# Six-pass graph network on one core: the attention passes' pipeline reordered to two slots a group, with two gathers fewer a pass

## What is computed

```
h = relu(layernorm(x));  q, k, v = h @ Wq + bq, h @ Wk + bk, h @ Wv + bv
a   = einsum(q[src], k[dst]) / sqrt(D)          # one score a head and edge
ex  = exp(a - segment_max(a, dst)[dst])
agg = segment_sum(v[src] * ex, dst) / segment_sum(ex, dst)
x   = x + prelu(layernorm(gate * skip + (1 - gate) * agg))
```

## Time and profile before

| | |
|---|---|
| median of 3 runs | 6951.99 us (6948.68 to 6959.38) |
| the profiled execution | 6951.92 us |
| its span | 6950.0 us |
| TensorE / weight loads / VectorE busy | 71% / 59% / 69% |
| ScalarE / GpSimd busy | 22% / 68% |
| granted TensorE clock, mean | 0.786 |

### The profile page before, as it was taken

How to read it: one execution, slowest core, us unless ns; L and a number is a source line. 1 busy time by engine, 2 the same in 40 slices (tenths; PEclk the granted TensorE clock), 3 DMA queues, 4 the chain that set the end, 5 groups by cost and what they waited for, 6 DMA issues and landing times. The chain is left out here.

```text
span 6950.0 us, 92236 instructions
## 1 busy us (share of the span) xinstructions
PE 4911.1 (71%) x26631; PEld 4085.5 (59%) x26631; DVE 4761.2 (69%) x14309; ACT 1562.0 (22%) x4929; POOL 4755.9 (68%) x5008
## 2 busy tenths in 40 slices
PE   2655555667766577777688888867888886667766
PEld 2444444556665465565466666656777775566665
DVE  4444443777877577877577777747777874788786
ACT  2433332222222111111112112111222221121121
POOL 3777776777776577777577666627777763777774
PEclk8666666777677788888799889968887886877776
DMA  4444445666666355555455555547766673666664
GB/s 133 165 164 158 159 164 146 204 216 210 214 217 180 125 161 167 166 155 167 121 171 179 167 164 175 168 121 228 242 229 229 231 219 134 215 226 220 223 226 138
DMA packets 408006, 1267.81 MB, mean 182 GB/s; under 512 B 128774, under 2 KB 189958, under 8 KB 321110
## 3 DMA queue, kind: packets, MB, share of 16 engines
q1 hardware_dynamic: 200000, 760.73, 30.7%
q0 software_dynamic: 200240, 496.31, 25.8%
q10 hardware_dynamic: 7270, 4.88, 0.3%
HBM read 1084.56 MB, written 176.98 MB: 182 GB/s over the span
## 5 line engine op out<-in xcount | busy, mean ns | idle before, releaser
L756 POOL DMA_INDIRECT gathered_rows<-table_l,arena x3056 | 2909.3, 952 | 1192.4 <-issue 904.2
L1298 PE MATMUL ps<-weighted_rows,onehot 128*128 128x136 f32 (+2 forms) x8320 | 1527.4, 341 | 573.9 <-DVE acc L1150 568.8
L1298 PEld LDWEIGHTS ps<-weighted_rows,onehot 128*128 128x128 f32 x8320 | 1353.3, 241 | 729.3 <-DVE weighted_rows L1139 334.1
L1260 PEld LDWEIGHTS ps<-dst_side,onehot_t 128*128 128x128 f32 x8320 | 1299.9, 232 | 384.1 <-issue 318.3
L756 POOL DMA_INDIRECT gathered_rows<-table_l,src_rel_edges x1120 | 1063.7, 950 | 603.5 <-issue 328.4
L1260 PE MATMUL ps<-dst_side,onehot_t 128*128 x8320 | 1381.4, 320 | 90.0 <-DVE products L1067 43.8
L1150 DVE TENSOR_TENSOR acc<-acc,ps 128x136 f32 (+2 forms) x4160 | 1185.9, 285 | 178.1 <-PE ps L1298 83.5
L1256 PE MATMUL ps<-gathered_rows,ident 128*128 128x512 f32 x832 | 547.3, 745 | 307.0 <-DMA gathered_rows<-table_l,arena 302.4
L1072 DVE TENSOR_REDUCE scores<-products 128x16 f32<-128x512 f32 (+2 forms) x1040 | 706.5, 679 | 10.0
L879 PE MATMUL ps<-gathered_rows,onehot 128*128 128x128 f32 x1664 | 346.3, 373 | 465.3 <-ACT gathered_rows L816 464.3
L756 POOL DMA_INDIRECT arena<-table_l,src_rel_edges x544 | 516.5, 950 | 180.2 <-issue 160.3
(11 more groups left out here) (322 smaller groups left out, 6029.5 us busy)
## 6 DMA issues: line engine op xcount, KB each, us to landing
onehot_t<-onehots_turned SPq DMA_DIRECT2D x260, 1024.0 KB
onehot<-onehots SPq DMA_DIRECT2D x260, 1024.0 KB
onehots<-onehot SPq DMA_DIRECT2D x52, 1024.0 KB, 6.8
onehots_turned<-onehot_t SPq DMA_DIRECT2D x52, 1024.0 KB, 4.3
table_l<-arena SPq DMA_DIRECT2D x50, 1024.0 KB
gathered_rows<-table_l,arena POOLq DMA_INDIRECT x3056, 2.5
segment_flags_sb<-segment_flags SPq DMA_DIRECT2D x1300, 8.2 KB
arena<-type_mask_rows SPq DMA_DIRECT2D x75, 256.0 KB
```

The source lines that it names most:

```text
L756: pool.indirect_dma_start(out=home(v, t // GC)[:, t % GC, :], out_offset=None, in_=table, in_offset=bass.IndirectOffsetOnAxis(ap=index[:, ...
L1260: ins = nc.tensor.matmul(ps[:, BZ + k, g * P:(g + 1) * P], e.ohT[:, u, t * P:(t + 1) * P], kRows[:, bass.ds(bs[t % 8], D)], start=not gat, ...
L1298: ins = nc.tensor.matmul(ps[:, BP + n % 3, at:at + PW], e.oh[:, u, t, :], exvT[:, t, :], start=True, stop=True)
```

## The change

- A group passes through two slots and the beginning of a third. VectorE's slot s holds the products and scores of group s, and of group s-1 the chain, maxima, rescale, weighing and adds 0 to 10; adds 11 to 15 of a group stand at the start of the next slot. The flag `weighs` and one drain slot go.
- ScalarE's `open_scale`, `exps` and `exp_columns` stand in a row, without a hook between them, and TensorE's `spread_drop` and `turn_back` likewise.
- TensorE forms all four chunks of destination rows of group s in slot s; if `gat`, the identity matmul of the gathered rows comes last and in a function of its own (`own_rows`), further down the list.
- `first(k)` becomes 8 (s + 1) + 6 for t < 11 and 8 (s + 2) otherwise.
- The last group gathers 14 tiles in place of 16; waits for its rows are lowered by as much.
- Register loads of eight places, two a slot on each of the two engines, as before; VectorE's second one is kept over to the next slot.

```diff
+LACK = NT - NT_MAX
+ON_TIME = SUMMED[3][1]
...
+def rows_wanted(s, j, q):
+
+    return 64 * (q + 1) - (16 * LACK if s == NG - 1 and j == J - 1 else 0)
+
...
-            for t in range(GT):
+            for t in range(min(GT, NT_MAX - s * GT)):
...
                     keep_scores(s - 1)
                 after.act(act, x)
-                after.act(act, x + 1)
                 if cur:
                     keep_column(s, u, q)
-                after.act(act, x + 2)
-                after.act(act, x + 3)
+                after.act(act, x + 1)
                 if chain:
                     open_scale(s - 1, 1 - u)
-                after.act(act, x + 4)
-                if chain:
                     exps(s - 1)
-                after.act(act, x + 5)
+                    exp_columns(s - 1)
+                after.act(act, x + 2)
+                for h in range(3, 7):
+                    after.act(act, x + h)
                 if cur:
                     keep_linear(s, w)
-                after.act(act, x + 6)
-                if chain:
-                    exp_columns(s - 1)
                 after.act(act, x + 7)
 
...
+            late_places = {}
+
+            def unit_of_adds(s, n, bs):
+                for t in range(*SUMMED[n]):
+                    add(s, t, bs[t % 8])
+
+            def slot(s, w, qw, cur=True, chain=True, late=True):
+
+                r, o = s - 1, s - 2
                 v, rq = two(*place(w, qw, ways, -1))
-                vp = (w - 2) % buffers
                 x = HOOKS * s
-                def late_adds(n, m):
-                    if late:
-                        for k in range(n, m):
-                            add(o, 8 + k, bb[k])
                 if late:
-                    bb = blocks_of(o, 8)
-                if late:
-                    e.p_ready.wait(dve, a_no, UNITS * (o + 1))
-                if weighs:
-                    e.excol_ready.wait(dve, a_no, p + 1)
-                    last_maxima(p)
-                    for j in range(J):
-                        weigh(p, vp, j)
-                after.dve(dve, x)
-                late_adds(0, 3)
+                    bo = late_places.pop(o)
+                    unit_of_adds(o, 4, bo)
                 if chain:
                     scan_tiles(r, v, rq)
-                late_adds(3, 5)
+                if late:
+                    unit_of_adds(o, 5, bo)
                 if chain:
                     turn_ends(r)
-                late_adds(5, 8)
+                after.dve(dve, x)
                 after.dve(dve, x + 1)
-                if weighs:
-                    bp = blocks_of(p, 0)
-                    rescale(p, w % 2, bp[0])
                 if chain:
                     chain_forward(r, v)
                 if cur:
                     product(s, w, qw, 0)
                 if chain:
                     chain_backward(r, v)
+                    hand_back_ends(r)
+                    open_drop(r)
+                    max_forward(r, v)
+                    max_backward(r, v)
+                    less_maximum(r)
+                if cur:
+                    score(s, 0)
                 if chain:
-                    hand_back_ends(r)
+                    br = blocks_of(r, 0)
+                    rescale(r, v, br[0])
                 after.dve(dve, x + 2)
                 if chain:
-                    open_drop(r)
-                if cur:
-                    score(s, 0)
-                if weighs:
-                    for t in range(3):
-                        add(p, t, bp[t])
+                    e.excol_ready.wait(dve, a_no, r + 1)
+                    last_maxima(r)
+                    for j in range(J):
+                        weigh(r, (w - 1) % buffers, j)
                 after.dve(dve, x + 3)
                 if cur:
                     product(s, w, qw, 1)
-                if weighs:
-                    add(p, 3, bp[3])
-                if cur:
                     score(s, 1)
+                if chain:
+                    unit_of_adds(r, 0, br)
                 after.dve(dve, x + 4)
                 if chain:
-                    max_forward(r, v)
-                    max_backward(r, v)
-                    less_maximum(r)
+                    unit_of_adds(r, 1, br)
+                    unit_of_adds(r, 2, br)
+                    bl = late_places[r] = blocks_of(r, 8)
                 after.dve(dve, x + 5)
-                if weighs:
-                    add(p, 4, bp[4])
                 if cur:
                     product(s, w, qw, 2)
-                if weighs:
-                    add(p, 5, bp[5])
-                if weighs:
-                    add(p, 6, bp[6])
-                if cur:
                     score(s, 2)
+                if chain:
+                    unit_of_adds(r, 3, bl)
                 after.dve(dve, x + 6)
-                if weighs:
-                    add(p, 7, bp[7])
                 if cur:
                     product(s, w, qw, 3)
                     score(s, 3)
@@ -1233,33 +1230,34 @@
...
+            slot(NG, NG % ways, NG // ways, cur=False)
+            slot(NG + 1, (NG + 1) % ways, (NG + 1) // ways, cur=False, chain=False)
...
             def dst_rows(s, w, qw, j, bs):
                 u, q = two(w, qw)
-                v, qv = buffer(w, qw)
                 c, k = J * s + j, j % 2
-                if gat:
-                    here[v][j].wait(pe, here_no, 64 * (qv + 1))
                 if not (static(s, 1) and j < 2):
 
                     e.prod_ready.wait(pe, a_no, c - 1)
-                if gat:
-
-                    nc.tensor.matmul(ps[:, BZ + k, :].rearrange("p (g d) -> p g d", d=D), e.ident[:, :], home(v, j)[:, :, 0:D],
-                                     start=True, stop=False)
                 for g in range(GC):
                     t = GC * j + g
                     ins = nc.tensor.matmul(ps[:, BZ + k, g * P:(g + 1) * P], e.ohT[:, u, t * P:(t + 1) * P],
-                                           kRows[:, bass.ds(bs[t % 8], D)], start=not gat, stop=not gat or g == GC - 1)
-                ins.then_inc(e.z_ready.sem, 1)
+                                           kRows[:, bass.ds(bs[t % 8], D)], start=not gat or g == 0, stop=not gat)
+                if not gat:
+                    ins.then_inc(e.z_ready.sem, 1)
+
+            def own_rows(s, w, qw, j):
+                v, qv = buffer(w, qw)
+                if gat:
+                    here[v][j].wait(pe, here_no, rows_wanted(s, j, qv))
+                    nc.tensor.matmul(ps[:, BZ + j % 2, :].rearrange("p (g d) -> p g d", d=D), e.ident[:, :], home(v, j)[:, :, 0:D],
+                                     start=False, stop=True).then_inc(e.z_ready.sem, 1)
...
-            def slot(s, w, qw, cur=True, chain=True, weighs=True, ahead=True):
-
-                r, p = s - 1, s - 2
-                u, pq = two(*place(w, qw, ways, -2))
-                wn, qn = place(w, qw, ways, 1)
+            def slot(s, w, qw, cur=True, chain=True):
+
+                r = s - 1
+                u, q = two(w, qw)
+                v, rq = two(*place(w, qw, ways, -1))
                 x = HOOKS * s
+                if cur:
+                    bs = blocks_of(s, 0)
+                    e.oht_here[u].wait(pe, a_no, 16 * (q + 1))
+                    dst_rows(s, w, qw, 0, bs)
+                if chain:
+                    turn_scores(r)
+                if cur:
+                    dst_rows(s, w, qw, 1, bs)
                 after.pe(pe, x)
-                if weighs:
-                    e.oh_here[u].wait(pe, a_no, 16 * (pq + 1))
+                if cur:
+                    own_rows(s, w, qw, 0)
+                after.pe(pe, x + 1)
+                if chain:
+                    spread_drop(r)
+                    turn_back(r)
+                after.pe(pe, x + 2)
                 if cur:
                     bs = blocks_of(s, 8)
-                if weighs:
-                    sums(p, u, 0)
-                after.pe(pe, x + 1)
-                if weighs:
-                    sums(p, u, 1)
-                    sums(p, u, 2)
-                after.pe(pe, x + 2)
-                if chain:
-                    spread_drop(r)
-                if cur:
                     dst_rows(s, w, qw, 2, bs)
                 after.pe(pe, x + 3)
-                if weighs:
-                    sums(p, u, 3)
+                if cur:
+                    own_rows(s, w, qw, 1)
+                if chain:
+                    e.oh_here[v].wait(pe, a_no, 16 * (rq + 1))
+                    for n in range(3):
+                        sums(r, v, n)
                 after.pe(pe, x + 4)
                 if cur:
                     dst_rows(s, w, qw, 3, bs)
+                if chain:
+                    sums(r, v, 3)
                 after.pe(pe, x + 5)
+                if cur:
+                    own_rows(s, w, qw, 2)
+                if chain:
+                    sums(r, v, 4)
+                    sums(r, v, 5)
                 after.pe(pe, x + 6)
```

(32 more changed lines are left out.)

29 lines of the change are left out of this document (14 added, 15 removed).

## The result

The changed kernel takes 7031.03 us (median of 4 runs, 7022.54 to 7034.22) against 6954.85 (6948.68 to 6959.38): a ratio of 1.0106, 95% interval 1.009 to 1.0122. It is slower by 76 us, where the forecast was 37 us faster, and it lies a microsecond above the range. The profiled execution is the fastest of the four, 7022.54 us with a span of 7020.8, 70.8 more than before.

What follows compares the result with a forecast made beforehand. GpSimd's gathers bound passes 1, 2 and 5, the VectorE, TensorE and ScalarE loop passes 3 and 4, with pass ends a second cost. Terms -10 - 96 + 10 + 0 + 59 = -37 us: 6952 to 6915 us, range 6790 to 7030.

Steps and rivals of the forecast that it cites:

- Two gathers fewer: Last group of a pass: rows come 2.5 us earlier in passes 0, 1, 2 and 5, -10 us; nothing in 3 and 4.
- One slot fewer at each end: End of passes 1 to 5, last product to last block's first read: 20 us each, -96 us in all.
- Adds and scores not interleaved: VectorE's slot: grouped adds and back-to-back scores cost 0.6 us more, hidden under the gathers in passes 1, 2 and 5.
- The sum: VectorE's work and waits added up per slot: pass 3 22.9 us, no change; pass 4 22.7, taken as 22.4.
- Exponentials without block work between: ScalarE and TensorE between maxima and weighing: about 1.3 us, covered by 1.4 to 1.6 of VectorE's work; costed at nothing.
- The drain that the prediction weighed and left out: ScalarE's table switch for the square root: about 1.38 us on top of the load, up to 58 us more in all.
- Destination rows ahead, own rows behind: Passes 2 and 3: one-hot part formed before gathered rows arrive, identity matmul closes the bank; same matmuls, costed at nothing.
- Block work in TensorE's list: Passes 3 and 4: projections and relations delay sums and scores; pass 4 slots 22.4 us, +59 us, pass 3 unchanged.
- the walk: Step-by-step count of pass 4's waits for sums and scores, all additive: 2.9 us a slot for 18 blocks, 1.8 for 7.
- the loop held by TensorE's list in every pass: Rival: each block-work matmul becomes a wait, passes 1, 2 and 5 at 20.6 us a slot; +96, 7048 us; chance 0.27.

Runs made afterwards that it cites:

- run 7: Changed kernel with the own rows' identity matmul opening the bank again and two adds put back between the third product and its score: 6888.29 us.
- run 2: Changed kernel with one part undone: the own rows' identity matmul opens the bank again, ahead of the one-hot matmuls: 6952.31 us.
- run 5: Changed kernel with twelve more one-hot matmuls a slot in passes 2 and 3, ahead of the spreading of the drop: 6992.22 us.
- run 10: The kernel of run 7 with pass 4's block work one place later for blocks whose last tile is below 11 in its group: 6857.28 us.
- Run 12: The kernel of run 10 with pass 4's key, value and query matmuls cut to the first of eight types: 6806.25 us.
- run 6: The kernel of run 2 with pass 4's block work shifted four to six places, to where TensorE waits for the drop: 6984.24 us.
- run 3: Changed kernel with two of VectorE's adds put back between the third product and its score: 7058.19 us.

## Why the prediction was wrong

1. *Two gathers fewer.* -2.5 us a pass was expected; pass 0 takes 1076.7 to 1084.9 us over the twelve runs and the changed kernel, and 1086.4 in the one trace of the kernel before. The sign fits; the size can't be told apart from that scatter. Not tried by itself.

2. *One slot fewer at each end.* Right. VectorE's timeline, last product and last block's first read, passes 1 and 4, as in the earlier trace rows:

```profile
2230.51 0.69 DVE L1076 TENSOR_TENSOR products<-gathered_rows,ps 128x512 f32<-128x512 f32 x1 [0.92 <-DMA gathered_rows<-table_l,arena]
...
2248.11 0.17 DVE L1775 TENSOR_SCALAR row_scalars<-acc 128x4 f32<-128x4 f32 x1
...
5863.98 0.68 DVE L1076 TENSOR_TENSOR products<-gathered_rows,ps 128x512 f32<-128x512 f32 x1
...
5886.56 0.17 DVE L2254 TENSOR_SCALAR row_scalars<-acc 128x8 f32<-128x8 f32 x1
```

17.6 and 22.6 us; 18.0, 22.1 and 18.9 in passes 2, 3 and 5 (before 35.4, 44.5 and 38.6). Together 99 us where 100 was said, 105 less than before where 96 was said. Passes 1, 3 and 5 show it whole.

3. *Adds and scores not interleaved.* The sign was right; the place was the wrong question. VectorE's busy time a slot of pass 1 is 848.26/51.9 = 16.3 us against 15.5 before, 0.8 more where 0.6 was said, and it stayed under the gathers in passes 1 and 5 as the step had it. (The step reads the earlier trace rows wrong in one place: with an add between, product and score start 4507.87 - 4507.07 = 0.80 apart; 0.60 is the product's share of it. The 0.12 a score that it goes on with is right.) What it missed is what stands ahead of the second register load. The sum counted both loads as work; with own rows early, a product, two adds and a score in place of five adds ahead of that load are worth 26 and 24 us in passes 3 and 4 (run 7), and the idle time that goes is the one behind the load. This is read from the waits; a kernel with only the load moved was not tried.

4. *Exponentials without block work between.* Right: VectorE's wait for ScalarE's columns during the gathers of pass 4 is 1.4 us, where it was 59.9. A square root stands ahead of the exponentials in this stretch of ScalarE's timeline:

```profile
5323.12 0.20 ACT L1476 ACTIVATE row_scalars<-row_scalars 128x1 f32<-128x1 f32 x1 [1.49 <-DVE row_scalars L1471]
5323.34 1.28 ACT L1023 ACT_TABLE_LOAD   x1
5325.25 0.27 ACT L1023 ACTIVATE open_node_scale<-ps,open_node_column 128x8 f32<-128x8 f32 x1 [0.62 <-PE ps L1274]
```

The load takes 1.28 us and ends 0.6 us before the spread drop comes, and the next activation starts 0.63 us after it. The drain that the prediction weighed and left out is longer than that, and is in no row; that the load is hidden here is read from this slot, and not tried by itself.

5. *Destination rows ahead, own rows behind: "I cost it at nothing".* **This step failed, by 52 us in pass 2 and 27.5 in pass 3** (run 2). I asked whether the gathered rows were there; they were. I did not ask when TensorE gets to the closing matmul, which stands in its list behind three things that VectorE and ScalarE release, and I took the matmuls to be "the same ones" in a place where they run at half the clock. GpSimd's pace was to cover pass 2, by 0.8 us a slot (19.3 under 20.1); the waits for the banks are 3.4 a slot (175.2/51), and the slot came out 1.3 over the gathers. That pass 3 came out right is luck. Its slot is 22.35 us as forecast, but without this part it is (4515.70 - 3408.22)/51 = 21.72 (run 2). VectorE's waits for banks, scores, scale and columns make some 3.6 us of the 22.35, where steps 5 and 6 had 2.7, so its own work is about 18.7 (an estimate from these waits), where the sum had 20.2: a wait left out and own work put too high cancelled. No row shows the 19.6 of that sum.

6. *Block work in TensorE's list.* The mechanism was right and its size too small: pass 4 slots of 23.63 us, not 22.4, +2.38 where +1.15 was said: 63 of the pass's 72 us. The own work in the sum, 20.1 us a slot, came out right: with the 3.6 us of waits below it makes 23.7. The two waits are where the step put them. It said 3.2 us for sums; the slot above shows 4.58. Over the pass, sums and scores make (140.7 + 44.7)/51 = 3.6 us a slot, and I had 2.6 from the walk and then took 0.3 off because a walk adds up what may overlap. One part of the difference is the clock: I took key and value at 3.84 us, they took 4.67 here, and 4.55 in the mean of the pass's 22 blocks with matmuls before the last gather (4.07 in the kernel before); the one-hot matmuls ahead of them took 2.07. The 0.3 off had no row behind it.

Of the rivals, the loop held by TensorE's list in every pass (7048) comes nearest in the total, but not in its passes: 1 and 5 never left the gathers' pace, at slots of 20.13 and 20.18, and 3 fell. It named the clock, which run 5 confirms for pass 2. What the forecast and this rival should have been is one case: new waits on TensorE's list in passes 2 to 4, and none that counts in 1 and 5. (Pass 5's busy time a slot, 813.65/51.9, is 15.7, not 15.6; nothing hangs on it.)

What stays open: after run 10, pass 4 is still 49 us longer than before, though its end is shorter. Run 12 puts a good part of that on the projections' total, and that VectorE's slot in the changed kernel has 0.8 us more work is measured; how the rest divides was not tried.

## What to carry to other kernels

When a step is split so that its first half goes ahead, price the second half where it now stands: list what its engine waits for ahead of it, and at which clock it runs afterwards. A piece of side work costs what the other engine's cover is short of its whole length, so it belongs behind what is waited for, or in pieces shorter than the gap; an idle stretch that is itself a wait for the critical chain is no free place (run 6). And a rewritten order is worth taking apart: here the shorter ends (105 us) were good, two other parts undone turned 76 us of loss into 67 of gain (run 7), and one place's shift made it 98 (run 10). A register load belongs behind a long instruction and not behind a short one: here that was 0.8 us of idle time a slot or 0.2.

## What the runs showed of the hardware that I had not expected

More matmuls, less time: 12 more a slot lifted the granted clock of pass 2 from 0.82 to 0.92, brought the 128x512 identity matmul from 759 to 681 ns in the mean and the pass from 1147.4 to 1100.1 us. A lower clock does not make a pass longer by itself: with 21 of 24 projection matmuls gone the clock of pass 4 fell from 0.77 to 0.75, and the pass was 92 us shorter.

A register load's idle time on VectorE depends on what runs ahead of it: 0.82 us behind an add of 0.30 us (changed kernel, at 5315.95), 0.20 us behind a score of 0.68 us (run 3, at 5323.47).
